# Self-attention of 16 heads: the next pair's products at other steps, and its weights loaded in pieces

## The reference

```python
def _L1_attn_ref(x, w_q, w_k, w_v, w_o):
    ...
    q = jnp.einsum('bsd,hqd->bhsq', x, w_q)
    k = jnp.einsum('bsd,hqd->bhsq', x, w_k)
    v = jnp.einsum('bsd,hvd->bhsv', x, w_v)
    scores = jnp.einsum('bhsq,bhtq->bhst', q, k)
    masked = jnp.where(causal, -jnp.inf, scores)
    weights = jax.nn.softmax(masked / jnp.sqrt(jnp.float32(dq)), axis=-1)
    out = jnp.einsum('bhst,bhtv->bhsv', weights, v)
    cat = out.transpose(0, 2, 1, 3).reshape(b, s, -1)
    return jnp.einsum('bsf,df->bsd', cat, w_o)
```

## Time and profile before

| | |
|---|---|
| median of 3 runs | 3018.18 us (3016.68 to 3021.74) |
| the profiled execution | 3010.78 us |
| its span, first to last instruction | 3008.8 us |
| TensorE busy | 2276.8 us (76%) |
| VectorE busy | 2175.1 us (72%) |
| ScalarE, GpSimd busy | 1060.2 us (35%), 585.9 us (19%) |
| the 16 DMA engines, mean over the span | queue q1: 41.4% |
| mean granted TensorE clock | 0.867 of full speed |

### The profile page before, as it was taken

How to read it: one execution, slowest core, us unless ns; L and a number is a source line. 1 busy time by engine, 2 the same in 40 slices (tenths; PEclk the granted TensorE clock), 3 DMA queues, 4 the chain that set the end, 5 groups by cost and what they waited for, 6 DMA issues and landing times.

```text
span 3008.8 us, 50636 instructions
## 1 busy us (share of the span) xinstructions
PE 2276.8 (76%) x17470; PEld 1830.6 (61%) x17470; DVE 2175.1 (72%) x4246; ACT 1060.2 (35%) x2004; POOL 585.9 (19%) x666
## 2 busy tenths in 40 slices
PE   3667788868776877886877687888677777888875
PEld 3556666657465756664755565666565566666663
DVE  6765788866866578885776667888586666788767
ACT  2312444422432244442242224444224223444324
POOL 2111222212101122221101112222120102222220
PEclk8778899989777889998877789999877878999988
DMA  6001689840001078983000119897100014899600
GB/s 234 1 15 40 137 160 171 154 86 1 1 15 56 15 149 161 170 152 63 1 1 15 56 37 167 166 164 144 31 1 15 1 55 85 161 169 166 113 1 14
DMA packets 658407, 251.39 MB, mean 84 GB/s; under 512 B 613082, under 2 KB 633946, under 8 KB 657370
## 3 DMA queue, kind: packets, MB, share of 16 engines
q1 hardware_dynamic: 653978, 243.79, 41.4%
q10 hardware_dynamic: 4160, 4.19, 0.4%
HBM read 52.87 MB, written 10.49 MB: 21 GB/s over the span
## 4 chain that ended last, share of the span: by engine, by line
issue 38%; PE 23%; DVE 18%; DMA 11%; ACT 5%; POOL 4%; DVEq 1%; ACTq 0%; SPq 0%; POOLq 0%
DMA l_ptb<-l_phb 6%; PE ps L233 5%; PE ps L235 5%; PE ps L234 4%; DMA l_pts<-l_phs 4%; DVE nmax L1385 3%; PE ps L1289 1%; DVE l_k L1440 1%; DVE l_q L1444 1%; DVE l_phb L1391 1%; DVE l_phs L1391 1%; ACT l_q L1351 1%; PE ps L1271 1%; ACT xn L1347 1%; POOL d_pn L990 1%
## 5 line engine op out<-in xcount | busy, mean ns | idle before, releaser
L1385 DVE TENSOR_REDUCE nmax<-ps 128x1 f32<-128x1024 f32 (+7 forms) x512 | 383.3, 750 | 23.0 <-PE ps L1273 20.9
L1494 POOL CAST l_phb<-l_pb 128x1024 f16<-128x1024 f32 (+3 forms) x256 | 241.4, 943 | 654.1 <-ACT l_pb L1336 337.8
L1336 ACT ACTIVATE l_pb<-ps,nmax 128x1024 f32<-128x1024 f32 (+3 forms) x256 | 244.7, 956 | 283.5 <-DVE nmax L1385 282.7
L1271 PE MATMUL ps<-l_k,l_q 128*128 128x512 f32 (+3 forms) x768 | 319.1, 416 | 24.3 <-ACT l_ps L1336 23.9
L1391 DVE TENSOR_TENSOR l_phb<-l_pb,l_phb 128x1024 f16<-128x1024 f32 (+3 forms) x256 | 288.2, 1126 | 15.5 <-POOL l_phb L1494 13.4
L1272 PE MATMUL ps<-l_k,l_q 128*128 128x512 f32 (+3 forms) x768 | 270.1, 363 | 0.0
L1289 PE MATMUL ps<-l_v,l_ptb 128*128 128x64 f16 x4992 | 197.8, 197 | 34.2 <-DMA l_ptb<-l_phb 34.1
L1289 PEld LDWEIGHTS ps<-l_v,l_ptb 128*128 128x128 f16 x4992 | 177.1, 101 | 67.4 <-DMA l_ptb<-l_phb 41.1
L233 PE MATMUL ps<-xTh,l_w 128*128 128x512 f32 x256 | 123.1, 481 | 83.9 <-DVE l_q L1444 50.5
L1494 POOL CAST l_phs<-l_ps 128x128 f16<-128x128 f32 (+3 forms) x256 | 124.2, 485 | 319.1 <-DMA l_pts<-l_phs 169.6
L1271 PEld LDWEIGHTS ps<-l_k,l_q 128*128 128x128 f32 x768 | 156.0, 203 | 44.2 <-ACT l_ps L1336 29.8
(11 more groups left out here) (361 smaller groups left out, 6279.4 us busy)
## 6 DMA issues: line engine op xcount, KB each, us to landing
l_k<-xn SPq DMA_DIRECT2D x128, 256.0 KB, 4.1
l_w<-l_wqk_s SPq DMA_DIRECT2D x32, 512.0 KB, 4.8
l_wv<-l_wv_s SPq DMA_DIRECT2D x16, 512.0 KB, 6.0
xin<-in_x SPq DMA_DIRECT2D x4, 1024.0 KB, 5.5
m_w<-in_m_w SPq DMA_DIRECT2D x8, 512.0 KB, 4.4
m_w<-in_m_w SPq DMA_DIRECT2D x4, 1024.0 KB, 9.2
l_wo<-in_l_wo SPq DMA_DIRECT2D x16, 256.0 KB, 4.5
l_ptb<-l_phb SPq DMA_TRANSPOSE x256, 4.1
```

Of the source, the lines that this page charges most:

```text
L1271: pe.matmul(s[:, c0:c1], q, L["l_k1"][:, h, c0:c1], start=True, stop=False)
L1336: s.activation(l_numer(k)[:, 0:n], l_banks(k)[:, 0:n], ACT.Exp, bias=nmax[:, k % 4:k % 4 + 1], accum_out=lsum[:, h, k % NT:k % NT + 1]).th ...
L1385: v.tensor_reduce(nmax[:, k % 4:k % 4 + 1], l_banks(k)[:, 0:n], AX.X, ALU.max, negate=True).then_inc(q_["max"], 1)
L1494: g.tensor_copy(l_parts(k)[:, 0:cols], l_numer(k)[:, 0:cols]).then_inc(q_["hi"], 1)
```

## The change

It does four things. (1) In `l_tasks` the second half of K moves from step 1 to step 4, the halves of Q from 4 and 5 to 6 and 8, and the four O or V tasks from 7, 9, 11, 13 to 10, 12, 14, 15. T stays at 2 and 3, the first half of K at 0, and what the last pair does is unchanged. (2) `l_load_w` becomes four DMAs of 128 KB at steps 2, 5, 8 and 13, `l_load_wv` two of 256 KB at steps 7 and 10, and their readers wait for 64 and 32 counts in place of 16. (3) `l_dup` moves from steps 4 and 10 to 6 and 11, `l_load_wo` from 2 to 9. (4) VectorE gets a wait in the C task of the last pair, for the copy of its keys (`dup1`), before it writes over their source. No computing instruction is added or removed.

```diff
--- before.py
+++ after.py
@@ -1138,17 +1138,17 @@
 
             if j == HP - 1 and k in CONTEXT:
                 return CONTEXT[k]
-            if k in (0, 1):
-                return ("K", j + 1, k) if j + 1 < HP else None
+            if k in (0, 4):
+                return ("K", j + 1, k // 4) if j + 1 < HP else None
             if k in (2, 3):
                 return ("T", j - 1, k - 2) if j >= 1 else None
-            if k in (4, 5):
-                return ("Q", j + 1, k - 4) if j + 1 < HP else None
-            if k in (7, 9, 11, 13):
+            if k in (6, 8):
+                return ("Q", j + 1, k // 2 - 3) if j + 1 < HP else None
+            if k in (10, 12, 14, 15):
                 if j % 2 == 0 and j >= 2:
-                    return "O", j // 2 - 1, (k - 7) // 2
+                    return "O", j // 2 - 1, (10, 12, 14, 15).index(k)
                 if j % 2 == 1 and j + 1 < HP:
-                    return "V", (j + 1) // 2, (k - 7) // 2
+                    return "V", (j + 1) // 2, (10, 12, 14, 15).index(k)
             return None
 
         FIRST_BANK = {("K", 0, 0): 2, ("K", 0, 1): 3, ("Q", 0, 0): 4, ("Q", 0, 1): 7,
@@ -1207,13 +1207,13 @@
             bank = ps[:, l_bank(t), :]
             if kind in "KQ":
                 if kind == "K" and g == 0:
-                    pe.wait_ge(q_[f"w{n % 2}"], (b * NQ + n // 2 + 1) * 16)
+                    pe.wait_ge(q_[f"w{n % 2}"], (b * NQ + n // 2 + 1) * 64)
                 m = "QK".index(kind)
                 for c in range(DC):
                     last = mm3(pe, bank, L["l_w"][:, n % 2, 0, m, c, :], L["l_w"][:, n % 2, 1, m, c, :], xTh[:, c, halves(g)], xTl[:, c, halves(g)], c == 0, c == DC - 1)
             elif kind == "V":
                 if g == 0:
-                    pe.wait_ge(q_["wv"], (b * NQ + n + 1) * 16)
+                    pe.wait_ge(q_["wv"], (b * NQ + n + 1) * 32)
                 for u in range(2):
                     tok = slice((2 * g + u) * P, (2 * g + u + 1) * P)
                     for c in range(DC):
@@ -1417,6 +1417,7 @@
                     v.tensor_scalar(X1["c_kT"][:, c, :], bank[:, c * CK:(c + 1) * CK], x1_bk[:, c:c + 1], None, ALU.add)
                     v.tensor_scalar(X1["c_vT"][:, c, :], bank[:, (2 + c) * CK:(3 + c) * CK], x1_bv[:, c:c + 1], None, ALU.add)
                 v.drain()
+                v.wait_ge(q_["dup1"], (b * HP + HP) * 32)
                 for src, dst in ((X1["c_kT"], l_kC), (X1["c_vT"], X1["c_vC"])):
                     for c in range(2):
                         last = v.tensor_tensor(dst[:, c, :].rearrange("p (h k) -> p h k", k=CK), src[:, c, :].unsqueeze(1).to_broadcast([P, 8, CK]),
@@ -1510,11 +1511,14 @@
             for o in (slice(0, 64), slice(64, 128)):
                 sp.dma_start(f32(L["l_k1"][o, h, :]), f32(l_x[mine, :])).then_inc(q_[f"dup{h}"], 16)
 
-        def l_load_w(sp, b, j):
-            sp.dma_start(f32(L["l_w"][:, j % 2]).rearrange("p l m c e -> p l (m c e)"), a["l_wqk_s"][:, :, j, :]).then_inc(q_[f"w{j % 2}"], 16)
-
-        def l_load_wv(sp, b, q):
-            sp.dma_start(f32(L["l_wv"][:]).rearrange("p l c e -> p l (c e)"), a["l_wv_s"][:, :, q, :]).then_inc(q_["wv"], 16)
+        def l_load_w(sp, b, j, part):
+
+            l, m = part // 2, part % 2
+            sp.dma_start(f32(L["l_w"][:, j % 2, l, m]).rearrange("p c e -> p (c e)"),
+                         a["l_wqk_s"][:, l, j, m * DC * P:(m + 1) * DC * P]).then_inc(q_[f"w{j % 2}"], 16)
+
+        def l_load_wv(sp, b, q, l):
+            sp.dma_start(f32(L["l_wv"][:, l]).rearrange("p c e -> p (c e)"), a["l_wv_s"][:, l, q, :]).then_inc(q_["wv"], 16)
 
         def l_load_wo(sp, b, q):
             sp.dma_start(L["l_wo"][:], a["l_wo"][2 * q:2 * q + 2].rearrange("m p d -> p m d")).then_inc(q_["wod"], 16)
@@ -1522,8 +1526,10 @@
         def l_sp(sp, b):
             sp.wait_ge(s_xu, b * (NPH * NT) + 2 * NT)
             for j in range(2):
-                l_load_w(sp, b, j)
-            l_load_wv(sp, b, 0)
+                for part in range(4):
+                    l_load_w(sp, b, j, part)
+            for l in range(2):
+                l_load_wv(sp, b, 0, l)
             l_load_wo(sp, b, 0)
             for h in range(2):
                 l_dup(sp, b, 0, h)
@@ -1533,17 +1539,19 @@
                 j, k = g // NB1, g % NB1
                 if g + 4 < NB:
                     l_flip(sp, b, g + 4)
-                if j + 1 < HP and k == 4:
+                if j + 1 < HP and k == 6:
                     l_dup(sp, b, j + 1, 0)
-                if j + 1 < HP and k == 10:
+                if j + 1 < HP and k == 11:
                     l_dup(sp, b, j + 1, 1)
-                if j + 2 < HP and k == 2:
-                    sp.wait_ge(*lower(b, ("Q", j + 1 - 1, 1)))
-                    l_load_w(sp, b, j + 2)
-                if j % 2 == 0 and j + 2 < HP and k == 2:
-                    sp.wait_ge(*lower(b, ("V", j // 2, 3)))
-                    l_load_wv(sp, b, j // 2 + 1)
-                if j % 2 == 1 and j >= 3 and k == 2:
+                if j + 2 < HP and k in (2, 5, 8, 13):
+                    if k == 2:
+                        sp.wait_ge(*lower(b, ("Q", j, 1)))
+                    l_load_w(sp, b, j + 2, (2, 5, 8, 13).index(k))
+                if j % 2 == 0 and j + 2 < HP and k in (7, 10):
+                    if k == 7:
+                        sp.wait_ge(*lower(b, ("V", j // 2, 3)))
+                    l_load_wv(sp, b, j // 2 + 1, (7, 10).index(k))
+                if j % 2 == 1 and j >= 3 and k == 9:
                     sp.wait_ge(*lower(b, ("O", j // 2 - 1, 3)))
                     l_load_wo(sp, b, j // 2)
```

## The result

The changed kernel takes 3193.23 us, median of 4 runs (3186.64 to 3203.96), against 3017.43 (3011.69 to 3021.74) of the kernel before beside it: a ratio of 1.0587 [1.0552 to 1.0622], 177 us slower. The profiled execution took 3203.96 us.

A forecast was written before the change was run, and what follows sets the result against it. No engine was full: TensorE and VectorE waited for each other through bank 5. 50 us gained ahead of K and Q, less 6 for the O and V chain, made 44 us less: 2974 us, range 2915 to 3030.

The forecast's parts named there:

- The copy of the keys ... must land by step 10: 4 steps of 2.5 us against 4.1 us; nothing.: Sync queue, copy moved from step 4 to 6: lands in time for step 10, cost nothing.
- The last piece leaves at step 13 and is needed 3 steps, 7.5 us, later.: Last `l_w` piece on the sync queue: lands in time, since even a whole load lands in 4.8 us.
- What shorter loads give the transposes I also put at 0: Transposes near the split loads: no gain counted, TensorE's work after whole loads being bound by Q's chain.
- cost 0 with an upper end of 54 us for the issues: Sync queue: 84 more DMA issues of 0.64 us fall mostly into SP's waits for VectorE.
- the slower rival: SP's queue becomes the last releaser, ready transposes standing behind issues of pieces: 3072 us, chance 0.16.
- The gain, 50 us.: VectorE's waits ahead of K and Q: 2.5 us a pair in place of 4.3, over 28 pairs.
- the chain's 6: O and V at 10, 12, 14, 15, K at 0 behind: delay to K seen by VectorE, 6 us more.
- the four waits on VectorE: Waits ahead of lower parts: K's first half 1.4 us, K's second 0.8, Q's first 0, Q's second 0.3.
- the prediction's own last sign of being wrong: Wrong if pairs of heads get shorter but VectorE's wait ahead of K and Q does not.
- The 0 for the first half of Q.: Q at step 6: VectorE's 3.07 us of own work covers 2.93 us, so 0 wait in place of 2.19.
- Q's second half two steps ahead of its scores.: TensorE stands about 1.5 us a pair, 42 us in all, costed at nothing because VectorE has other work.
- The wait in the C task, at nothing.: VectorE's added wait in the C task: its copy left 5 steps before, 12 us against 4.1, no cost.

The follow-up runs named there:

- Products alone: Kernel before with K, Q, O and V tasks at the changed steps, whole sync queue as before, C-task wait kept: 2991.9 us, 0.9913 of the kernel before.
- both: Changed kernel with the copy of head 0's keys back at step 4 and the last `l_w` piece at step 9: 3008.1 us, 0.9971 of the kernel before.

## Why the prediction was wrong

The sum of 44 us was for one half of the change. The other half was costed at nothing, term by term, and two of these terms hold the result.

- *"The copy of the keys ... must land by step 10: 4 steps of 2.5 us against 4.1 us; nothing."* This is the step that failed first. It measured 105 us in the new order and 74 in the old. The 4.1 us of the earlier trace rows were right for one DMA; the copy is two, and took 5.4. The 4 steps of 2.5 us weren't: the queue is at step 6 when VectorE is there, and TensorE needs the keys in its turn 10, which it reaches two turns sooner. Between 534.17, the issue, and 534.78, where TensorE was ready for the scores, 0.6 us was left.
- *"The last piece leaves at step 13 and is needed 3 steps, 7.5 us, later."* The same mistake, 86 us. Of the 7.5 us 0.2 was left in the timeline above, against a landing of 3.1.
- *"What shorter loads give the transposes I also put at 0"*, and cost 0 with an upper end of 54 us for the issues. The number of DMAs costs 12 us, inside these bounds. The place is worth 58 to 62 us in the old order of the products (70 less the 12; the whole loads at 8); in the new one number, place and smaller moves come to 17 together. The sum didn't price it. Only the slower rival names it, a transpose that is ready behind a piece at steps 5 to 13, and prices it by the issues alone.
- *The gain, 50 us.* "Products alone" gave 26, so the sign held and the size was off by half; the 44 after the chain's 6 is outside its interval, 17 to 35 us. The working doesn't hold. Of the four waits on VectorE it put at 1.4, 0.8, 0 and 0.3 us, the timeline of "products alone" shows, near 455 to 486 us, 1.44, 1.64, 0.65 and 2.35. In batch 0 they are 34.7 us in all, where 18 were forecast and 30.4 stood before; over the span they didn't fall by 50 us but rose by 17. That is the prediction's own last sign of being wrong, shorter pairs without a shorter wait ahead of K and Q. What shrank instead are the waits for transposes and rounding, for which nothing had been counted. "I count gains on VectorE, not on TensorE" was the choice that failed here.
- *The 0 for the first half of Q.* It takes VectorE's own 3.07 us of work as cover for the 2.93 us from task to lower part. But ScalarE has an exponential ahead of its copy of Q, and that one waits for a maximum out of this same work:

```profile
458.81 0.47 ACT L1336 ACTIVATE l_ps<-ps,nmax 128x256 f32<-128x256 f32 x1 [3.27 <-DVE nmax L1385]
...
459.27 1.18 ACT L1351 ACTIVATE l_q<-ps 64x512 fp32r<-64x512 f32 x2
```

  TensorE began the task at 456.01; ScalarE stood until VectorE had the maximum, and VectorE could start at 460.49, 4.48 us after the task and after 0.65 us of idling. So work of VectorE up to that maximum doesn't cover the wait; it moves the copy back. For the second half the task itself began late, behind a wait of 1.31 us for a transpose, and ran at the lower clock (0.63 us a matmul where 0.40 is usual).
- *"6 us more" for O and V.* In the new order nothing of it can be measured, but alone on the old one the move costs 46 us: the parts aren't additive, and a price for each by itself, as the sum has it, can't be given.
- *Q's second half two steps ahead of its scores.* Right in size: 1.5 us a pair were forecast, 1.46 stand in the timeline of "products alone" before the scores (1.56 in the pair above), and 26.5 us in all against an end of 42. VectorE's waits for scores fell all the same (20.9 to 13.5 us), so nothing shows that it was paid.
- *The wait in the C task, at nothing.* Right: 0.5 us of idling stand behind it.
- *The slower rival.* Its end of 3072 us is over a hundred short, and in the changed kernel its mechanism isn't the one: waits for transposes fell to 8.0 us, and by its own sign SP should hardly wait any more, and it still waits for VectorE for 594.2 us, against 587.5 in the earlier trace rows:

```profile
SPq L1504 <- DVE l_phs L1391: 370.5, 185, 11.9
...
SPq L1504 <- DVE l_phb L1391: 223.7, 110, 4.1
```

Nor were the issues longer than thought. Landing and issue after the change, from the page and from the view of line 1517 (ns min/median/max):

```profile
l_k<-xn SPq DMA_DIRECT2D x128, 256.0 KB, 4.1
l_w<-l_wqk_s SPq DMA_DIRECT2D x128, 128.0 KB, 3.1
l_wv<-l_wv_s SPq DMA_DIRECT2D x32, 256.0 KB, 3.4
```

```profile
L1517 SPq DMA_DIRECT2D l_w<-l_wqk_s x128: 323/587/1322, 227.5 to 2951.8; - x128
```

The rule on small transfers, cited in the prediction from the Trainium skill ("DMA: Bandwidth & Descriptors", sections "Bandwidth" and "Anatomy of one DMA"), gave an estimate of 168 us, close to the 177 measured, by luck. The kernel with all the pieces at step 2 has the same transfers and loses 12 us, and "both" has as many, with the gain of the products, and is at 0.9971.

## What to carry to other kernels

A step number in a software pipeline is a different time for each engine. For a transfer that moves, find in the timeline when its queue gets there (what does the instruction ahead of it wait for, and at which turn is that engine?) and when the reader gets there, and compare these two, not the step numbers. Moving a load out of a quiet place into one where the queue works for the critical path has a price even when it lands in time; and when a change has several parts, run each alone and all but one, since here one part hid a gain and two parts that lose alone gain together.

## What was not expected of the hardware

- A stand of TensorE cost twice here. After 4.80 us of idling the granted clock went from 1.00 (2.4 GHz) to a mean of 0.69 over 8 us, so that part of them ran at the other level, 1.2 GHz, and work of 1.95 us took 3.60. Over the span the mean clock is 0.841 against 0.867, and TensorE's busy time 76 us higher with the same instructions.
- The landing of these loads grows far less than their size: 3.1 us for 128 KB of `l_w` and 4.8 for 512 KB before, 3.4 for 256 KB of `l_wv` and 6.0 for 512 KB before, issued right behind `l_w`; 256 KB of `l_k` take 4.1. So does the issue: a quarter of the size took 0.59 us at the median against 0.70.
- One DMA transpose occupied the queue for 1.20 to 3.96 us in the rows above, so that what is behind it moves by as much.
